# A graph network's tensor product laid out contiguously, with PSUM operands in the scoring and placing stages

## The chip, the cores and the metric

One core of a Trainium2 chip runs the whole kernel. The metric is the device time of one execution in microseconds (us). The kernel before takes 12370.3 us, the median of three runs (12365.73 to 12378.43).

The engines are named as in the profile: PE (TensorE, with its weight loads as PEld), DVE (VectorE), ACT (ScalarE), POOL (GpSimd) and SP (SyncE). POOL issues the indirect DMAs; SP and ACT issue the plain ones.

## The reference, cut to what matters

Four graph layers work on 12500 nodes with 32 features and on 200000 edges sorted by `dst`. Before each layer `h = relu(layernorm(x))`, and the layer's result is added to `x`.

```
# layer 0: scores of edges, two heads of 32
en, ev = (h @ W2s + b2s)[src], (h @ W2d + b2d)[dst]
e      = sum(leaky_relu(en + ev, 0.2) * attn, -1)
alpha  = softmax of e over the edges of one dst
msg    = softmax(en * r_feat * alpha, -1)
x     += (h + sum over heads(segment_sum(msg, dst))) @ W1 + b1
# layer 1
x     += segment_sum(h[src], dst)
# layer 2: weights of a tensor product per edge, MUL = 8
tpw = silu(silu(radial @ W1 + b1) @ W2 + b2) @ W3 + b3      # 4 blocks of 8 x 8: W00, W110, W01, W10
m0  = a * (einsum('eu,euw->ew', hs*sh0, W00) + einsum('eui,ei,euw->ew', hv, sh1, W110)/sqrt(3))
m1  = a * (einsum('eu,ei,euw->ewi', hs, sh1, W01) + einsum('eui,euw->ewi', hv*sh0, W10))
x  += self terms + segment_sum([m0, m1], dst) / 4
# layer 3: attention with four heads over the edges of one src
```

Layer 3 sums over `src`, so the kernel also puts the edges in the order of `src`.

## The kernel before, in words

The 200000 edges are padded to 128 x 1568: partition p holds 1568 edges that follow each other. An edge stage goes through them in 98 chunks of 16 columns (CH = 16), two chunks k = 0, 1 to a turn of the loop, each with its own buffers. A stage is a block of five programs, one per engine, which wait for each other by semaphores that count chunks. The order of the work is written out by hand in each `body`. Stages don't overlap. Each gather or scatter of one column is one indirect DMA on POOL's queue, 16 for a chunk and 1568 for a stage.

**Scoring stage (lines 809 to 1000).** POOL gathers rows of `tab_s0` (L864) into `en`; SP stores them (L850); ACT loads them back (`bring`, L876) with the rows of `dst`, which are written once per node (L645) and spread over the edges of the node by a running scan (`Spread`, L623 to 677). DVE first counts `dst` with one-hot comparisons against a row of iotas (`count_dst`, `hot`, L938 and L940), which PE adds up; from that come the positions that L645 needs (`starts`). POOL gathers 12 turns before it waits for them. Then DVE's loop (L981) makes, for each chunk, the one-hot rows of `src`, the scan (L675), the add (L988), the leaky ReLU (L989), the product with `attn` (L990) and the sum (L991). POOL's loop waits for the loaded indices and for SP's store two chunks before, not for DVE.

**Placing stage (L1003 to L1273).** DVE multiplies `en` by `r` (L1233), weights it (L1239), takes a softmax per head (maximum L1244, subtraction L1248, ACT's exponential, sum L1199, product L1203), adds the heads into `fresh` (L1207) and scans (L603). In the same loop PE ranks the edges by `src` from one-hot rows (`hot`, L1191 and L1193), DVE picks the ranks (L1217), and POOL scatters the edge's ends to their place (L1060). DVE's `send` waits until the scatters of two chunks before have landed, as it writes their buffers; POOL waits for `posed` (L1227).

**Sum stage (L1333 to L1440).** POOL gathers `tab_h` rows (L1314), ACT turns them into `fresh`, which is in PSUM here, and DVE scans. The weights of layer 2 are prepared beside it.

**Tensor-product stage (L1449 to L1696).** The same L1314 gathers `tab_h` rows; PE makes the 256 weights of each edge in four quarters of a chunk (L1526 and L1527, double buffered in `tp_ps`); DVE multiplies them in PSUM by the edge's vectors (`prod_a` L1661, `prod_b` L1664) and reduces (`res_a` L1647, `res_b` L1649). `prod_b` is laid out so that its reduction reads with a step of 8 elements. `prepare` and `dot` make the vectors `zv` (L1621), `zz` (L1623, L1631) and `hv1` (L1624); ACT widens `zv` (L1578) and copies `hs` (L1574). The messages are added in turned order into `fresh` in SBUF (L1688, L1692) and scanned (L603) a chunk later. POOL waits for `prepared` and `widened` of two chunks before.

**Attention stage (L1850 to L1963).** POOL gathers `tab_h3` rows (L1876); the message `fresh`, and with it one input of the long scan, is in PSUM.

Of the kernel before, what the change touches and what calls it, by code (L numbers as in the profile page):

```python
# [113 lines left out]
def known_ge(t, n):  # L114

    return isinstance(t, int) and t >= n
# [15 lines left out]
def build(nc, A, out):  # L132
    top = ExitStack()
    with top:
# [115 lines left out]
        class EdgeMasks:  # L250
# [11 lines left out]
            def scratch(self, st, ends=None):  # L262
# [12 lines left out]
                self.rows = ps(st, "rows", [128, 2, 512])  # L275
# [346 lines left out]
        class Spread:  # L622
# [4 lines left out]
            def __init__(self, st, width, table, masks):  # L627
                self.masks = masks
                self.width, self.whole, self.table = width, table, edge_rows(table[0:EDGES, :])
                self.raw = [sb(st, f"raw{k}", [EP, CH, width]) for k in range(2)]  # L630
                self.fresh = [sb(st, f"sfresh{k}", [EP, width, CH + 1]) for k in range(2)]
                self.keep = [sb(st, f"skeep{k}", [EP, width, CH + 1]) for k in range(2)]
                self.run = [sb(st, f"srun{k}", [EP, width, CH + 1]) for k in range(2)]
# [18 lines left out]
            def start(self):  # L652

                for k in range(2):
                    last = nc.vector.memset(self.keep[k][:, :, 0], 0.0)
                return [last, nc.vector.tensor_copy(self.run[1][:, :, CH], self.init[:, :])]
# [5 lines left out]
            def lay(self, act, t, k, i):  # L662
# [4 lines left out]
                K.wait(act, "act", self.raw_in[k], i * 16 + 16)  # L667
                nc.scalar.copy(self.fresh[k][:, :, 1:CH + 1], self.raw[k][:, :, :].rearrange("p c f -> p f c")).then_inc(self.laid, 1)  # L668

            def scan(self, dve, c, t, k):  # L670

                c.step(nc.vector.tensor_copy(self.fresh[k][:, :, 0], self.run[1 - k][:, :, CH]))
# [4 lines left out]
                K.wait(dve, "dve", self.spread, t + 1)  # L677

# [130 lines left out]
        with ExitStack() as st:  # L809
# [7 lines left out]
            zw = sb(st, "zw", [EP, CH, 64])  # L817
# [6 lines left out]
            cnt_ps = [ps(st, f"cnt_ps{k}", [NP, NB]) for k in range(2)]  # L824
            tot_ps = ps(st, "tot_ps", [NP, NB])
            pre_ps = ps(st, "pre_ps", [NP, NB])
            ev = Spread(st, 64, ev_rows, by_dst)
            by_dst.scratch(st, dst_ends)
# [5 lines left out]
            cleared, scored, hots, counted, copied, summed, starts, chain_v, loaded = (  # L834
                K.sem(n) for n in ("cleared", "scored", "hots", "counted", "copied", "summed", "starts", "chain_v", "loaded"))
# [37 lines left out]
            def _(act):  # L873
# [32 lines left out]
            def _(pe):  # L906
                by_dst.turn(pe)
                for q in range(2):
                    nc.tensor.matmul(cnt_ps[q][:, :], zbias[:, :], zbias[:, 0:NB], start=True, stop=False)
# [1108 lines left out]
```

## Time and profile before

| What | Value |
|---|---|
| Median of three runs | 12370.3 us |
| Profiled execution | 12366.65 us, its span 12364.9 us |
| POOL busy | 9229.0 us, 75% of the span |
| DVE busy | 6714.3 us, 54% |
| PE, PEld, ACT busy | 3621.8, 2317.2, 3298.7 us |
| L1314 indirect DMAs, two stages | 3136, 3142.1 us, mean 1002 ns |
| L864 indirect DMAs, scoring | 1568, 2088.0 us, mean 1332 ns |
| L1060 indirect DMAs, placing | 1568, 1933.5 us, mean 1233 ns |
| L1876 indirect DMAs, attention | 1568, 1481.3 us, mean 945 ns |

Times of rows are from one profiled execution. A POOL row of an indirect DMA is the time in which POOL works on the instruction; 0.30 us lie between two of them. DVE rows that follow each other overlap by about 0.1 us, so the busy time of a stretch is less than the sum of its rows.

### The profile page before, as it was taken

What the parts mean: (1) busy time and instruction counts of PE and PEld (TensorE: products, weight loads), DVE (VectorE), ACT (ScalarE), POOL (GpSimd) and SP (SyncE); (2) the same over time, 40 slices, a digit from 0 to 9 for tenths busy, and PEclk for the clock granted to TensorE, in tenths of its full rate; (3) what the DMA queues carried; (4) which work ended last, traced back from release to release, by engine and by line L of the source; (5) the groups of instructions that cost most, each with busy time, mean ns of one, the idle gap of its engine ahead of it and who ended that gap; (6) DMA issues with size and microseconds to landing.
All of it is one profiled execution on the core that took longest, in us unless ns stands there. A gap on an engine that the chain in (4) does not pass through costs nothing. (4 is left out here: it accounts for less than half of the span.)

```text
span 12364.9 us, 102503 instructions
## 1 busy us (share of the span) xinstructions
PE 3621.8 (29%) x22342; PEld 2317.2 (19%) x22342; DVE 6714.3 (54%) x9984; ACT 3298.7 (27%) x4609; POOL 9229.0 (75%) x8449
## 2 busy tenths in 40 slices
PE   3201000004555555510000000778887710000002
PEld 2200000003555545510000000233333210000001
DVE  8628754547666666630000001999999914444443
ACT  0002111113444444411111110333333303343332
POOL 5878877774777777767777776777777667777775
PEclk6555555556777777755555555888888755555555
DMA  6123322221111111111111111111111112222222
GB/s 231 41 61 112 96 82 88 83 85 52 52 56 52 54 53 52 56 22 27 26 26 27 26 26 33 27 27 27 27 27 27 25 14 71 71 71 74 71 71 60
DMA packets 596616, 683.05 MB, mean 55 GB/s; under 512 B 341381, under 2 KB 437478, under 8 KB 583766
## 3 DMA queue, kind: packets, MB, share of 16 engines
q0 software_dynamic: 270016, 149.13, 7.8%
q10 hardware_dynamic: 116464, 346.86, 7.6%
q1 hardware_dynamic: 210086, 186.52, 5.0%
q8 instruction: 16, 0.26, 0.0%
q14 instruction: 34, 0.28, 0.0%
HBM read 371.16 MB, written 310.60 MB: 55 GB/s over the span
## 5 line engine op out<-in xcount | busy, mean ns | idle before, releaser
L1314 POOL DMA_INDIRECT hs<-tab_h,idx x3136 | 3142.1, 1002 | 1047.1 <-issue 987.1
L864 POOL DMA_INDIRECT en<-tab_s,idx x1568 | 2088.0, 1332 | 582.8 <-issue 489.3
L1060 POOL DMA_INDIRECT by_src<-ends,pos_i x1568 | 1933.5, 1233 | 630.1 <-issue 495.1
L1876 POOL DMA_INDIRECT hs<-tab_h,idx x1568 | 1481.3, 945 | 511.8 <-issue 511.8
L1526 PE MATMUL tp_ps<-w_pair,x 128*128 128x512 f32 x1568 | 1010.3, 731 | 273.2 <-DVE prod_b L1664 272.9
L592 DVE COPY fresh<-run 128x32 f32<-128x32 f32 (+1 forms) x392 | 109.9, 280 | 1783.2 <-ACT fresh L1401 1768.4
L916 PE MATMUL cnt_ps<-hot_hi,hot_lo 128*128 128x98 bf16 x3136 | 287.3, 281 | 2409.2 <-DVE hot_hi L940 2409.2
L603 DVE TENSOR_TENSOR_SCAN run<-keep,fresh 128x544 f32<-128x544 f32 (+1 forms) x392 | 851.7, 2173 | 89.2 <-DVE fresh L592 58.3
L614 ACT COPY rows<-run 128x512 f32<-128x512 f32 (+1 forms) x392 | 706.9, 1803 | 516.0 <-DVE run L603 516.0
L916 PEld LDWEIGHTS cnt_ps<-hot_hi,hot_lo 128*128 128x128 bf16 x3136 | 250.6, 140 | 2445.9 <-issue 2059.1
L666 ACT COPY skeep<-cont_dst 128x1024 f32 (+1 forms) x98 | 102.4, 1045 | 2147.7 <-issue 2113.8
L1082 PE MATMUL rank_ps<-place_sb,hot_t 128*128 128x98 f32 x3136 | 661.6, 323 | 9.7 <-DVE picked L1217 9.4
L675 DVE TENSOR_TENSOR_SCAN srun<-skeep,sfresh 128x1088 f32<-128x1088 f32 (+1 forms) x196 | 268.3, 1369 | 685.1 <-ACT sfresh L668 653.2
L1757 PE MATMUL turn<-ident,both 128*33 128x128 f32 x8 | 1.9, 418 | 2155.4 <-DVEq L1787 2155.4
L1649 DVE TENSOR_REDUCE res_b<-prod_b 128x96 f32<-128x768 f32 x392 | 600.1, 1531 | 0.0
L529 PE MATMUL turn<-ident,tails 128*32 128x128 f32 x3 | 1.2, 394 | 2042.1 <-DMA tails<-sums 2042.1
L1082 PEld LDWEIGHTS rank_ps<-place_sb,hot_t 128*128 128x128 f32 x3136 | 542.3, 217 | 12.9 <-DVE picked L1217 6.6
L1137 ACT COPY hot_tb<-turn_ps 128x512 bf16<-128x512 bf16 x392 | 232.6, 593 | 1162.9 <-PE turn_ps L1072 1081.0
L1401 ACT COPY fresh<-hs 128x512 f32<-128x512 f32 x98 | 99.7, 1017 | 1409.5 <-DMA hs<-tab_h,idx 1409.5
L1941 DVE COPY score<-most 128x4 f32<-128x4 f32 x98 | 20.0, 204 | 838.7 <-DMA hs<-tab_h,idx 838.7
L1072 PE MATMUL turn_ps<-identb,hot_lo 128*128 128x128 bf16 x1568 | 174.4, 243 | 1016.7 <-DVE hot_hi L1193 1016.7
L1757 PEld LDWEIGHTS turn<-ident,both 128*33 128x33 f32 x8 | 1.2, 169 | 2155.7 <-DVEq L1787 2155.5
(327 smaller groups left out, 12998.4 us busy)
## 6 DMA issues: line engine op xcount, KB each, us to landing
sums<-rows ACTq DMA_DIRECT2D x98, 1088.0 KB
sums<-rows ACTq DMA_DIRECT2D x294, 256.0 KB
hs<-tab_h,idx POOLq DMA_INDIRECT x4704, 2.4
ev_rows<-zeros ACTq DMA_DIRECT2D x16, 3136.0 KB, 9.9
en_rows<-en SPq DMA_DIRECT2D x98, 512.0 KB
en_back<-en_rows ACTq DMA_DIRECT2D x98, 512.0 KB, 3.8
raw<-ev_rows ACTq DMA_DIRECT2D x98, 512.0 KB
en<-en_rows SPq DMA_DIRECT2D x98, 512.0 KB
```

Source lines behind the costliest of these rows:

```text
L603: nc.vector.tensor_tensor_scan(flat(self.run[k]), flat(self.keep[k]), flat(self.fresh[k]), 0.0, ALU.mult, ALU.add).then_inc(self.scanned, 1)
L614: nc.scalar.copy(self.rows[k][:, :, 0:self.width], self.run[k][:, :, 1:CH + 1].rearrange("p f c -> p c f")).then_inc(self.copied, 1)
L675: nc.vector.tensor_tensor_scan(flat(self.run[k]), flat(self.keep[k]), flat(self.fresh[k]), 0.0, ALU.mult, ALU.add).then_inc(self.spread, 1)
L864: pool.indirect_dma_start(en[k][:, g, :], None, tab_s0, bass.IndirectOffsetOnAxis(ap=idx[k][:, g:g + 1], axis=0)).then_inc(gathered[k], 16)
L916: last = nc.tensor.matmul(cnt_ps[q][:, :], hot_lo[k][:, g, :], hot_hi[k][:, g, :], start=False, stop=False)
L1060: pool.indirect_dma_start(by_src, bass.IndirectOffsetOnAxis(ap=pos_i[k][:, g:g + 1], axis=0), ends[k][:, g, :], None).then_inc(sent[k], 16)
L1082: nc.tensor.matmul(o, hot_t[q][:, b, :], place_sb[q][:, :], start=True, stop=False)
L1137: nc.scalar.copy(hot_tb[q][:, :, :], turn_ps[q % 2][:, :, 0:EP])
L1314: pool.indirect_dma_start(rows[k][:, g, :], None, tab_h, bass.IndirectOffsetOnAxis(ap=idx[k][:, g:g + 1], axis=0)).then_inc(gathered[k], 16)
L1526: nc.tensor.matmul(o, x2[k][:, a, b * EP:(b + 1) * EP], w3[:, :, :].rearrange("p o n -> p (o n)"), start=True, stop=False)
L1649: c.link(nc.vector.tensor_reduce(res_b[:, four, :, :].rearrange("p c i w -> p (c i) w"), prod_b[q % 2][:, :, :, :, :].rearrange("p c i u w ...
L1876: pool.indirect_dma_start(rows[k][:, g, :], None, tab_h3, bass.IndirectOffsetOnAxis(ap=idx[k][:, g, 1:2], axis=0)).then_inc(gathered[k], 16)
```

## The change

Three things are changed together.

*Scoring stage.* `zw` moves to PSUM. The row of iotas is copied to a PSUM tile once, as f32, and the comparisons read it there. `Spread` gets a form with one PSUM tile that is `fresh` and `run` at once for both chunks: the scan writes over its input, `free` carries the last column to the first, and ACT lays the next chunk only after that (`freed`). The leaky ReLU is split: ACT multiplies `zw` by 0.2 into `fifth` (`added`, `tilted`), and DVE takes the maximum. The comparisons of a chunk move behind the add. To have the banks, the counts share one bank, as do `tot_ps` and `pre_ps`, and the edge masks use `zw`'s.

*Placing stage.* A PSUM tile of one bank holds the iotas, `z_top`, `z_div` and a copy of the chunk's weights. `turn_ps` has one buffer instead of two. The heads are added by a reduction over the head instead of an addition.

*Tensor-product stage.* The weights `w3` and `b3` are turned once, so that an edge's 256 weights come as [w][block][u]. Both products and all reductions then read and write contiguously: `prod_a` is [w][24], `prod_b` is [w][i][u] and is made from `zv` without the widened copy. `res_a` is split into a reduction that writes m0 directly and one for `res_p`. The message is added in plain order into `msg`, and ACT turns it into `fresh` (`lay`). `prepare` moves to the end of a chunk, and PE's order of transposition, hidden layers and products changes.

```diff
@@ class Spread
+                if psum:
+                    held = ps(st, "sheld", [EP, -(-width * (CH + 1) // 512) * 512])
+                    whole = held[:, 0:width * (CH + 1)].rearrange("p (f c) -> p f c", c=CH + 1)
+                    self.fresh = self.run = [whole, whole]
+                    self.freed = K.sem("spread_freed")
...
+                if self.psum:
+                    K.wait(act, "act", self.freed, t + 1)
                 nc.scalar.copy(self.fresh[k][:, :, 1:CH + 1], self.raw[k][:, :, :].rearrange("p c f -> p f c")).then_inc(self.laid, 1)
...
+            def free(self, dve):
+                nc.vector.tensor_copy(self.fresh[0][:, :, 0], self.run[0][:, :, CH]).then_inc(self.freed, 1)
@@ scoring: ACT, then DVE
+                        K.wait(act, "act", added, t + 1)
+                        nc.scalar.mul(fifth[:, :, :], zw[:, :, :], 0.2).then_inc(tilted, 1)
                         if not known_ge(t, 2 * PAIRS - 1):
                             ev.lay(act, t + 1, 1 - k, i + k)
...
-                    nc.vector.tensor_tensor(hot_lo[k][:, :, :], iota_row[0:EP, :].unsqueeze(1).to_broadcast([EP, CH, 128]),
+                    nc.vector.tensor_tensor(hot_lo[k][:, :, :], iota_ps[:, 0:128].unsqueeze(1).to_broadcast([EP, CH, 128]),
...
-                        hot(lo_s, hi_s, t, k)
                         ev.scan(dve, c, t, k)
                         K.wait(dve, "dve", back_in[k], i * 16 + 16)
                         c.step(nc.vector.tensor_tensor(zw[:, :, :], en_back[k][:, :, :], ev.rows(k), ALU.add))
-                        c.step(nc.vector.scalar_tensor_tensor(zw[:, :, :], zw[:, :, :], 0.2, zw[:, :, :], ALU.mult, ALU.max))
+                        dve.sem_inc(added, 1)
+                        ev.free(dve)
+                        hot(lo_s, hi_s, t, k)
+                        K.wait(dve, "dve", tilted, t + 1)
+                        c.step(nc.vector.tensor_tensor(zw[:, :, :], zw[:, :, :], fifth[:, :, :], ALU.max))
@@ placing
+            small_ps = ps(st, "small_ps", [EP, 512])
+            per_edge = lambda at: small_ps[:, at:at + CH * HEADS0].rearrange("p (c h) -> p c h", h=HEADS0)
+            iota_ps, z_top, z_div, weight = small_ps[:, 0:128], per_edge(128), per_edge(160), per_edge(192)
...
-                    K.wait(pe, "pe", turned_sb, n - 1)
+                    K.wait(pe, "pe", turned_sb, n)
...
-                    c.link(nc.vector.tensor_tensor(S.message(k), z[k][:, :, 0:FEAT].rearrange("p c f -> p f c"),
-                                                   z[k][:, :, FEAT:2 * FEAT].rearrange("p c f -> p f c"), ALU.add))
+                    c.link(nc.vector.tensor_reduce(S.message(k), z[k][:, :, :].rearrange("p c (h f) -> p f c h", h=HEADS0), AX.X, ALU.add))
@@ tensor product: ACT
+                def lay(t, k):
+                    K.wait(act, "act", messaged, t + 1)
+                    K.wait(act, "act", S.scanned, t - 1)
+                    nc.scalar.copy(S.message(k), msg[k][:, :, :].rearrange("p c f -> p f c")).then_inc(laid, 1)
@@ tensor product: DVE
+                            a, b = prod_a[q % 2], prod_b[q % 2]
+                            c.link(nc.vector.tensor_reduce(msg[k][:, four, 0:MUL], a[:, :, :, 0:2 * MUL], AX.X, ALU.add))
+                            c.link(nc.vector.tensor_reduce(res_p[:, four, :], a[:, :, :, 2 * MUL:3 * MUL], AX.X, ALU.add))
+                            return c.mark(nc.vector.tensor_reduce(res_q[:, four, :].rearrange("p c n -> p (c n)"),
+                                                                  b[:, :, :, :].rearrange("p n i u -> p (n i) u"), AX.X, ALU.add))
...
+                        nc.vector.tensor_tensor(msg[k][:, :, MUL:FEAT], cross[:, :, :, :].rearrange("p c w i -> p c (w i)"),
+                                                res_q[:, :, :], ALU.add).then_inc(messaged, 1)
+                        if more:
+                            prepare(c, t + 1, 1 - k, i + k)
```

## Rows read from the trace of the kernel before

**Rows 1.** The page's first part: busy us, share of the span, instructions.
```profile
PE 3621.8 (29%) x22342; PEld 2317.2 (19%) x22342; DVE 6714.3 (54%) x9984; ACT 3298.7 (27%) x4609; POOL 9229.0 (75%) x8449
```

**Rows 2.** Stretches, POOL's gathers alone: length, busy; scoring twice, sum stage.
```profile
92.00:722.00 630.00, 508.77 (x384) 0.50 0.37 126
849.00:2800.00 1951.00, 1578.62 (x1184) 0.50 0.31 92
...
5534.00:7517.00 1983.00, 1482.83 (x1568) 0.50 0.13 27
```

**Rows 3.** Stretches, all engines: PE, PEld, DVE, ACT, POOL; counting, placing, tensor product.
```profile
112.00:495.00 383.00, 142.34 (x1555) 124.25 (x1556) 382.68 (x196) 0.00 (x0) 322.89 (x195) 0.50 0.44 159
2934.00:5363.00 2429.00, 1381.66 (x13928) 1237.09 (x13927) 1627.14 (x4562) 1168.06 (x2224) 1933.47 (x1568) 0.77 0.17 52
7687.00:9846.00 2159.00, 1737.72 (x4391) 673.93 (x4391) 2054.27 (x2416) 720.32 (x878) 1659.22 (x1568) 0.86 0.13 27
```

**Rows 4.** Timeline in scoring: start, duration, engine, line.
```profile
1602.83 2.29 DVE L938 TENSOR_TENSOR hot_lo<-iota_row,lo_s 128x2048 bf16<-128x2048 bf16 x1 [0.54 <-remote]
1603.31 2.63 POOL L864 DMA_INDIRECT en<-tab_s,idx  x1 [0.30 <-issue]
...
1625.27 0.94 POOL L864 DMA_INDIRECT en<-tab_s,idx  x1 [0.30 <-issue]
1625.43 1.23 DVE L990 TENSOR_TENSOR zw<-zw,attn 128x1024 f32<-128x1024 f32 x1
```

**Rows 5.** Timeline in the tensor-product stage; `fresh` in SBUF.
```profile
8601.17 1.28 DVE L603 TENSOR_TENSOR_SCAN run<-keep,fresh 128x544 f32<-128x544 f32 x1
8601.36 1.85 POOL L1314 DMA_INDIRECT hs<-tab_h,idx  x1 [0.30 <-issue]
```

**Rows 6.** Timeline in the attention stage; `fresh` in PSUM.
```profile
11016.98 4.83 DVE L603 TENSOR_TENSOR_SCAN run<-keep,fresh 128x2244 f32<-128x2244 f32 x1 [0.28 <-DVE fresh L592]
11017.72 0.94 POOL L1876 DMA_INDIRECT hs<-tab_h,idx  x1 [0.30 <-issue]
```

**Rows 7.** Timeline in the placing stage, POOL and DVE alone.
```profile
4023.12 1.29 DVE L603 TENSOR_TENSOR_SCAN run<-keep,fresh 128x544 f32<-128x544 f32 x1 [0.29 <-DVE fresh L1207]
4023.99 1.20 POOL L1060 DMA_INDIRECT by_src<-ends,pos_i  x1 [0.30 <-issue]
4025.24 1.22 DVE L1233 TENSOR_TENSOR z<-en,r 128x1024 f32<-128x1024 f32 x1 [0.82 <-remote]
4025.49 1.81 POOL L1060 DMA_INDIRECT by_src<-ends,pos_i  x1 [0.30 <-issue]
4027.61 0.97 POOL L1060 DMA_INDIRECT by_src<-ends,pos_i  x1 [0.30 <-issue]
```

**Rows 8.** Stretches, scoring's reduction L991 alone: length, busy, count of chunks.
```profile
850.00:1420.00 570.00, 50.07 (x41) 0.50 0.36 111
850.00:2820.00 1970.00, 119.68 (x98) 0.50 0.31 92
```

**Rows 9.** Instruction groups by line and shape: busy us, mean ns of one, idle before.
```profile
L1649 DVE TENSOR_REDUCE res_b<-prod_b 128x96 f32<-128x768 f32 x392 | 600.1, 1531 | 0.0
L1647 DVE TENSOR_REDUCE res_a<-prod_a 128x96 f32<-128x768 f32 x392 | 368.6, 940 | 0.0
L938 DVE TENSOR_TENSOR hot_lo<-iota_row,lo_s 128x2048 bf16<-128x2048 bf16 x98 | 224.6, 2292 | 65.3 <-remote 64.5 <-DVE zw L990 0.5
L668 ACT COPY sfresh<-raw 128x1024 f32<-128x1024 f32 x98 | 190.7, 1946 | 298.7 <-DMA raw<-ev_rows 298.7
L1692 DVE TENSOR_TENSOR fresh<-cross,res_b 128x384 f32<-128x384 f32 x98 | 107.2, 1094 | 0.0
L1207 DVE TENSOR_TENSOR fresh<-z 128x512 f32<-128x512 f32 x98 | 102.9, 1050 | 0.0
```

**Rows 10.** Waits of DVE in the placing stage: us in total, times, longest.
```profile
DVE ends L1223 <- DMA by_src<-ends,pos_i: 641.4, 95, 9.9
```

**Rows 11.** The page's DMA issues: KB each, median us from issue to landing.
```profile
en_back<-en_rows ACTq DMA_DIRECT2D x98, 512.0 KB, 3.8
```

More of the change, by code:

```diff
@@ L260, in __init__, with scratch @@
                 self.fwd_all = sb(top, "fwd_all_" + name, [128, EP])
-            def scratch(self, st, ends=None):
+            def scratch(self, st, ends=None, rows=None):
                 self.ends = ends
@@ L655, in start @@
                     last = nc.vector.memset(self.keep[k][:, :, 0], 0.0)
-                return [last, nc.vector.tensor_copy(self.run[1][:, :, CH], self.init[:, :])]
+                first = self.fresh[0][:, :, 0] if self.psum else self.run[1][:, :, CH]
+                return [last, nc.vector.tensor_copy(first, self.init[:, :])]
             def load(self, eng, t, k):
@@ L1024, in build @@
             place_ps = ps(st, "place_ps", [NP, NB])
-            turn_ps = [ps(st, f"turn_ps{k}", [NP, GR, 128], BF16) for k in range(2)]
+            turn_ps = ps(st, "turn_ps", [NP, GR, 128], BF16)
             own_ps = ps(st, "own_ps", [EP, GR, EP])
@@ L1324, in build @@
         w2 = sb(weights, "w2_pair", [128, 128])
-        w3 = sb(weights, "w3_pair", [128, 2, TPW])
+        w3 = sb(weights, "w3_pair", [128, 2, MUL, 4, MUL])
         b1 = sb(weights, "b1_pair", [128, 1])
@@ L1493, in body @@
                         K.wait(pool, "pool", prepared, t - 1)
-                        K.wait(pool, "pool", widened, t - 1)
+                        K.wait(pool, "pool", copied_hs, t - 1)
                         gather(pool, t, k, i)
@@ L1583, in _ @@
                 layer2(0, 0)
-                widen(0, 0, 0)
+                copy_hs(0, 0, 0)
+                S.mask(act, 0, 0)
                 def body(i):
@@ L1639, in body @@
                         c, last_c = chains[k], chains[1 - k]
-                        K.wait(dve, "dve", widened, t + 1)
+                        more = not known_ge(t, 2 * PAIRS - 1)
                         def total(q, done):
@@ L1668, in body @@
+                            nc.vector.tensor_tensor(
+                                prod_b[q % 2][:, :, :, :],
+                                wts[:, :, :, 3 * MUL:].rearrange("p c w u -> p (c w) u").unsqueeze(2).to_broadcast([EP, 4 * MUL, 3, MUL]),
+                                zv[k][:, four, :, :].rearrange("p c i u -> p c (i u)").unsqueeze(2).to_broadcast([EP, 4, MUL, 3 * MUL]),
+                                ALU.mult).then_inc(taken, 1)
                             if q == 1:
                                 last_c.restart()
-                            if q == 1 and not first_chunk(t):
-                                S.scan(dve, c, t - 1, 1 - k, carried=True, settle=False)
@@ L1684, in body @@
-                        crossed = c.mark(nc.vector.tensor_tensor(cross[:, :, :, :], sh1(t), res_a[:, :, :, 2].unsqueeze(3).to_broadcast([EP, CH, MUL, 3]), ALU.mult))
-                        msg = S.message(k)
+                                if not first_chunk(t):
+                                    K.wait(dve, "dve", laid, t)
+                                    S.scan(dve, c, t - 1, 1 - k, carried=True, settle=False)
+                            if q == 0:
+                                K.wait(dve, "dve", laid, t - 1)
+                            else:
+                                summed[q - 1] = total(q - 1, made[q - 1])
```

211 lines of the change are left out of this document (102 added, 109 removed).

## Prediction

> **What bounds the kernel now.** I read the page's first part, then a table of engine times for each stage, then the instruction groups of the POOL queue, then the timeline around the long members of those groups. POOL is busy 75% of the span, VectorE 54% [rows 1]. POOL's work is 98 chunks of 16 indirect DMAs in each of five stages: gathering for scoring (L864), scattering in the placing stage (L1060), gathers of the sum stage and of the tensor-product stage (both L1314), and of the attention stage (L1876). The 1568 gathers of the sum stage need 1983 us [rows 2], 1.26 us each and 20.2 us a chunk. They need 630 + 1951 = 2581 us in scoring [rows 2], 2429 us in placing and 2159 us in the tensor-product stage [rows 3]. So in three stages POOL is slower than its own clean pace, and nothing in its rows says that it waited: the rows are longer.
>
> The timeline shows why. A gather is 0.94 us. The one that starts at 1603.31, inside the VectorE comparison of 1602.83 to 1605.12, lasts 2.63 us and ends 0.82 us after it; the one at 1625.27, which has already begun when a product starts at 1625.43, lasts 0.94 us [rows 4]. The scan at 8601.17 stretches the gather at 8601.36 to 1.85 us [rows 5]. What these VectorE rows share is two inputs in SBUF. In the attention stage the scan of 4.83 us takes one input from PSUM, and a gather that starts inside it lasts 0.94 us [rows 6]. So a VectorE instruction with two SBUF inputs holds POOL at a point some 0.1 us into an indirect DMA until it ends; one with an input in PSUM does not.
>
> The excess is the difference of POOL's busy times over the same 1568 instructions: scoring 508.8 + 1578.6 - 1482.8 = 605 us [rows 2]; tensor product 1659.2 - 1482.8 = 176 us [rows 2, 3]; placing, whose unheld scatter is 0.97 us [rows 7], 1933.5 - 1568 x 0.969 = 414 us.
>
> **The change, part by part. Scoring.** The one-hot comparisons read the iota from PSUM, the scan works in place in one PSUM tile, the add reads its result there, and the leaky ReLU becomes an ACT product into SBUF and a maximum of that with PSUM. Every large VectorE instruction of the loops then has a PSUM input, in the first counting loop too. Of the 605 us I keep 5 us for the mask scans before the loops and take 600. POOL waits there for nothing of VectorE but `starts`. The counting loop costs 3.9 us a chunk (383 us for 98) [rows 3] and ends at 495; POOL reaches the placing of rows at 722 minus its excess of 508.8 - 384 x 0.945 = 146, about 580, so `starts` is still early. VectorE then begins scoring 146 us sooner, at about 704, and while it is behind it does 41 chunks in 570 us, 13.9 us each [rows 8]: 704 + 98 x 13.9 = 2066, before POOL's end at 2800 - 600 = 2200. POOL stays the bound up to 15.3 us a chunk. The added ACT product (1024 elements, at most the 1.95 us of the turned copy L668 [rows 9]) stands beside the comparisons, which are now issued behind the add: 4 us of them stand between the add and the maximum. Only in the last chunk are they exposed, since they used to run while its data was fetched: +4 us. Net -596.
>
> At one place a rule of the Trainium skill would speak against this. The all-bf16 comparison of 2048 elements takes 2292 ns, 1.12 ns an element [rows 9]; the f32 product of 1024 elements takes 1.22 us [rows 7], 1.19 ns an element, so the bf16 one has no faster mode now. VectorE: DVE Perf Modes, section "Why PSUM operands drop a tier", has it that an operand in PSUM takes the faster modes away from an instruction; by that rule the pair of comparisons would cost twice as much if it ran in such a mode now. By the row it doesn't, and the sum has 0 for it; the doubled pair is priced as a rival below.
>
> **Placing.** The comparisons, the weighting, the subtraction of the maximum and the division get a PSUM input, the head sum becomes a reduction with one input, and a small copy of the weights is added. Two holders are left: the product L1233 and the scan L603. In the timeline they cost 1.20 - 0.97 = 0.23 and 1.81 - 0.97 = 0.84 us [rows 7]. The 0.23 is luck of phase: other holders ran just in front. Against a stream with a point every 1.27 us, a lone holder of 1.29 us costs 0 to 1.29, 0.65 on average; one of 1.22 us that follows by 0.83 us then costs 0.8. I take 1.45 us a chunk, 142 us, between 50 (both fall well) and 210 (both fully). Saved: 414 - 142 = 272.
> VectorE must follow. It waits 641 us for landed scatters in this stage, 6.5 us a chunk [rows 10]; its loop is 2429 / 98 = 24.8, less 6.5, 18.3 us. The weights' copy adds 0.2. The head sum of 1024 strided elements replaces 1.05 us [rows 9]; strided reduction of 768 elements costs 1.53 us (L1649), contiguous 0.94 (L1647) [rows 9], so 1024 cost 1.2 to 2.1; I take 2.0. Loop: 19.5 us, against POOL's (2429 - 272) / 98 = 22.0. POOL keeps the bound by 2.5 us. The single turn_ps costs nothing: each transposition waits for ACT's copies of the group before, issued a group earlier.
>
> **Tensor product.** VectorE is busy 2054 / 98 = 21.0 us a chunk, in a stage whose chunk is 22.0 [rows 3]. The strided reduction goes from 1.53 to 0.94 us, four times: -2.4. Splitting the other into 512 and 256 elements adds four fixed parts of about 0.1: +0.4. The strided message add of 1.09 us [rows 9] becomes a contiguous one of about 0.55, and the add of a third as many elements beside it goes, by the same row some 0.36: -0.9. VectorE: 18.1. But POOL was nearly the bound already: 20.2 clean + 1.8 excess = 22.0. So VectorE's 3 us are worth only what they let POOL have. The scan (both inputs in SBUF, up to 1.29) stays; the long add is replaced by a short one; the products of `prepare` and the cross product stay. Per chunk: scan 0.65, the short ones 0.65, together 1.3 (0.4 to 2.2) against 1.8: -0.5 x 98 = -49. ACT loses the widened copy and gains the turned message copy; both lie beside. The stage's tail (last landing to last scan) is one VectorE chunk either way: -1. Extra weight turning in the sum stage is hidden by its gathers: 0. Net -50.
>
> **Sum**, on the profiled execution's 12366.65 (span 12364.9 and 1.75 around it): -596 - 272 - 50 = -918, 11449. The median before is 3.6 above that execution: 11452.
>
> **Rivals.**
> (a) Holders left over fall well: 50 us in placing (-92 more), 0.5 us a chunk in the tensor product (-78 more): 11282. For it: scan 0.23 [rows 7]. Against: the two are adjacent and cannot both be missed often. 0.10.
> (b) VectorE, or its chain with PE and ACT, becomes the bound: placing at 24 us a chunk (reduction dearer, turn_ps serialising) gives 98 x 2.0 = +196; tensor product gains nothing, +50: 11698. For it: margins of 2.5 us; PE is busy 1738 us of 2159 there [rows 3]. Against: waits of VectorE for PE are almost absent. 0.10.
> (c) The comparisons double (the page's rule above): counting ends at 878, `starts` holds POOL until 885 instead of 580, and scoring runs at 13.9 + 4.1 = 18.0: 885 + 124 (placing rows) + 98 x 18 = 2773 against a forecast of 2220: +553; placing at 23.6, +157: 12162. Against: rows 9. 0.03.
> (d) The change doesn't do what it says: a PSUM input doesn't release POOL for comparisons whose other input is broadcast from SBUF, or in-place writing holds it. Then only about 50 is gained, and 4 lost: 12324. Against: rows 6. 0.03.
> (e) Slower: scoring has one tile where there were two for input and two for result, so scan, add, freeing, ACT's product, ACT's copy and the fetch of the next chunk can become one serial ring, with ACT standing behind its own `bring`. Fully serial: VectorE 13.9 + three ACT instructions of at most 1.95 + fetch 3.8 [rows 11] + store, taken the same, 3.8 = 27.4 us a chunk: 704 + 98 x 27.4 = 3389, 569 after the 2820 of now [rows 8]; less 272 and 50: 12617. It makes the kernel slower from (2820 + 322 - 704) / 98 = 24.9 us a chunk. Against: the next chunk's copy needs only add and freeing, so ring and comparisons overlap. 0.03.
> (f) The forecast: 0.71, with 11370 to 11540 of its own.
>
> A measurement tells 0.2%, 25 us, from no change. Faster: (a), (b), (c), (d), (f), 0.96 after something for what I overlook; same 0.01; slower 0.03. The range reaches over most of (a)'s and part of (b)'s way: 11330 to 11600.
>
> **What would show it.** Right: L864 at 0.95 us in the mean, L1060 near 1.06, the tensor product's gathers near 1.03; no gather stretched by a row with a PSUM input; VectorE idle on gathered rows in the tensor product, 3 us a chunk; its wait for scatters in placing down from 641 to about 250 us. Wrong: POOL rows of 0.95 us with idle time on `posed`, `prepared` or `starts` between (b, c, e), comparisons of over 2.3 us (c), long gathers inside comparisons (d).

## The result, and the profile after

The kernel after takes 11331.1 us (median of four runs, 11329.1 to 11339.1) against 12374.3 for the kernel before on the same chip: the ratio is 0.916, with a 95% interval of 0.914 to 0.918. It saves 1043 us; the forecast was 918, and its own range 11370 to 11540 was missed by 39 us, the wide one (11330 to 11600) reached by 1 us.

The page's first part and its groups of POOL's indirect DMAs, after (lines have moved: L864 is L881, L1060 is L1086, L1314 is L1342):

```profile
PE 3517.1 (31%) x22342; PEld 2369.0 (21%) x22342; DVE 6460.4 (57%) x10384; ACT 3225.0 (28%) x4707; POOL 8175.6 (72%) x8449
...
L1342 POOL DMA_INDIRECT hs<-tab_h,idx x3136 | 3035.4, 968 | 1046.2 <-issue 997.0
L1086 POOL DMA_INDIRECT by_src<-ends,pos_i x1568 | 1587.1, 1012 | 654.6 <-issue 513.8
L881 POOL DMA_INDIRECT en<-tab_s,idx x1568 | 1486.5, 948 | 590.6 <-issue 492.3
```

POOL is busy 9229.0 - 8175.6 = 1053 us less [rows 1], and the kernel is 1043 us shorter, with as many instructions on POOL. Scoring's gathers fell from 1332 to 948 ns in the mean, the scatters from 1233 to 1012.

Stretches of after in the order of [rows 3], all engines: scoring, placing, tensor product. After the length come PE, PEld, DVE, ACT and POOL, then the granted clock of PE as a share of 2.4 GHz, the busy share of the DMA engines and GB/s.

```profile
90.00:2206.00 2116.00, 288.39 (x3124) 251.63 (x3125) 1507.49 (x1013) 366.08 (x290) 1582.38 (x1667) 0.50 0.40 124
2344.00:4448.00 2104.00, 1387.73 (x13931) 1241.20 (x13928) 1726.15 (x4658) 1169.81 (x2224) 1587.11 (x1568) 0.81 0.20 60
6772.00:8823.00 2051.00, 1635.60 (x4398) 726.24 (x4398) 1788.36 (x2715) 568.25 (x878) 1552.35 (x1568) 0.85 0.13 28
```

| Stage: first to last indirect DMA | before, us | after, us | saved | forecast |
|---|---|---|---|---|
| scoring | 2707.0 | 2114.9 | 592 | 600 |
| gap from there to placing | 134.8 | 138.6 | -4 | -4 |
| placing | 2428.9 | 2103.1 | 326 | 272 |
| tensor product | 2158.1 | 2050.1 | 108 | 49 |
| from there to the attention stage's first gather | 331.0 | 324.3 | 7 | 1 |

The sum and attention stages kept 1982 and 1993 us. These differences add up to 1029 us, and the spans of the two profiled executions, 12364.9 and 11337.4, differ by 1028. The medians differ by 1043, because the execution profiled before lies 8 us under its kernel's median and the one profiled after 8 us over it.

Timeline of after in scoring (start, duration, engine, line), the place that answers to [rows 4]:

```profile
1812.94 2.43 DVE L686 TENSOR_TENSOR_SCAN sheld<-skeep,sheld 128x1088 f32<-128x1088 f32 x1 [1.23 <-ACT sheld L678]
1813.66 0.94 POOL L881 DMA_INDIRECT en<-tab_s,idx  x1 [0.30 <-issue]
...
1817.14 2.29 DVE L958 TENSOR_TENSOR hot_lo<-iota_ps,lo_s 128x2048 bf16<-128x2048 f32 x1
1817.41 0.94 POOL L881 DMA_INDIRECT en<-tab_s,idx  x1 [0.30 <-issue]
1818.65 0.94 POOL L881 DMA_INDIRECT en<-tab_s,idx  x1 [0.30 <-issue]
```

The gather that starts inside the scan of 2.43 us and the two inside the comparison of 2.29 us last 0.94 us, where the comparison of before made one of 2.63.

Timeline of after in placing, POOL and DVE alone, an odd chunk (the second of a turn of the loop) and an even one (the first of a turn), for [rows 7]:

```profile
3304.94 1.29 DVE L603 TENSOR_TENSOR_SCAN run<-keep,fresh 128x544 f32<-128x544 f32 x1 [0.36 <-DVE fresh L1234]
3305.78 1.23 POOL L1086 DMA_INDIRECT by_src<-ends,pos_i  x1 [0.30 <-issue]
3306.68 1.22 DVE L1260 TENSOR_TENSOR z<-en,r 128x1024 f32<-128x1024 f32 x1
3307.32 1.42 POOL L1086 DMA_INDIRECT by_src<-ends,pos_i  x1 [0.30 <-issue]
...
3327.69 1.29 DVE L603 TENSOR_TENSOR_SCAN run<-keep,fresh 128x544 f32<-128x544 f32 x1 [0.29 <-DVE fresh L1234]
3328.14 1.62 POOL L1086 DMA_INDIRECT by_src<-ends,pos_i  x1 [0.30 <-issue]
3330.06 0.97 POOL L1086 DMA_INDIRECT by_src<-ends,pos_i  x1 [0.30 <-issue]
3330.07 1.25 DVE L1260 TENSOR_TENSOR z<-en,r 128x1024 f32<-128x1024 f32 x1
```

In the odd chunk z<-en,r starts 0.45 us after the scan's end and stretches a scatter by 0.45 us. In the even one it starts 1.09 us after the scan's end, 0.01 us behind a scatter, which stays at 0.97.

Timeline of after in the tensor product, for [rows 5]:

```profile
7615.58 1.28 DVE L603 TENSOR_TENSOR_SCAN run<-keep,fresh 128x544 f32<-128x544 f32 x1
7616.03 1.58 POOL L1342 DMA_INDIRECT hs<-tab_h,idx  x1 [0.30 <-issue]
```

Groups of after by line and shape (busy us, mean ns), for [rows 9]:

```profile
L1691 DVE TENSOR_REDUCE res_q<-prod_b 128x96 f32<-128x768 f32 x392 | 369.2, 942 | 0.0
L1689 DVE TENSOR_REDUCE msg<-prod_a 128x32 f32<-128x512 f32 x392 | 263.0, 671 | 0.0
L958 DVE TENSOR_TENSOR hot_lo<-iota_ps,lo_s 128x2048 bf16<-128x2048 f32 x98 | 224.1, 2287 | 0.0
L1234 DVE TENSOR_REDUCE fresh<-z 128x512 f32<-128x1024 f32 x98 | 190.0, 1939 | 0.0
L1690 DVE TENSOR_REDUCE res_p<-prod_a 128x32 f32<-128x256 f32 x392 | 159.9, 408 | 0.0
L1008 DVE TENSOR_TENSOR zw<-en_back,sheld 128x1024 f32<-128x1024 f32 x98 | 120.5, 1229 | 28.7 <-DVE sheld L686 28.7
L1727 DVE TENSOR_TENSOR msg<-cross,res_q 128x384 f32<-128x384 f32 x98 | 55.0, 561 | 0.0
```

Waits of DVE in after: us in total, times, longest. The first is of the placing stage, for [rows 10], the others of the tensor product:

```profile
DVE ends L1249 <- DMA by_src<-ends,pos_i: 215.4, 52, 7.5
...
DVE hv L1667 <- DMA hs<-tab_h,idx: 127.2, 78, 32.2
DVE prod_a L1704 <- PE tp_ps L1566: 88.4, 133, 1.1
```

### The profile page after: what moved, and what is told of

It is laid out like the page before. It is cut to its first block and busy times, and to the rows that moved or that the text cites. A ratio compares the mean times of both kernels' runs of the same rounds, so it can differ in the third digit from the quotient of the medians.

```text
span 11337.4 us, 103348 instructions
## 1 busy us (share of the span) xinstructions
PE 3517.1 (31%) x22342; PEld 2369.0 (21%) x22342; DVE 6460.4 (57%) x10384; ACT 3225.0 (28%) x4707; POOL 8175.6 (72%) x8449
## 5 line engine op out<-in xcount | busy, mean ns | idle before, releaser
L1342 POOL DMA_INDIRECT hs<-tab_h,idx x3136 | 3035.4, 968 | 1046.2 <-issue 997.0
L1086 POOL DMA_INDIRECT by_src<-ends,pos_i x1568 | 1587.1, 1012 | 654.6 <-issue 513.8
L881 POOL DMA_INDIRECT en<-tab_s,idx x1568 | 1486.5, 948 | 590.6 <-issue 492.3
L1913 POOL DMA_INDIRECT hs<-tab_h,idx x1568 | 1481.4, 945 | 511.7 <-issue 511.7
L1565 PE MATMUL tp_ps<-w_pair,x 128*128 128x512 f32 x1568 | 905.4, 661 | 6.5 <-DVE prod_b L1707 6.5
L1549 PE MATMUL hid_ps<-radial_t,w_pairs 128*128 128x128 f32 x1568 | 357.4, 420 | 413.5 <-ACT radial_t L1597 413.5
L1704 DVE TENSOR_TENSOR prod_a<-tp_ps,zz 128x768 f32<-128x768 f32 x392 | 374.3, 955 | 136.6 <-PE tp_ps L1566 90.1
L1549 PEld LDWEIGHTS hid_ps<-radial_t,w_pairs 128*128 128x128 f32 x1568 | 333.0, 323 | 439.9 <-issue 421.3
```

The source lines that it names most:

```text
L881: pool.indirect_dma_start(en[k][:, g, :], None, tab_s0, bass.IndirectOffsetOnAxis(ap=idx[k][:, g:g + 1], axis=0)).then_inc(gathered[k], 16)
L1086: pool.indirect_dma_start(by_src, bass.IndirectOffsetOnAxis(ap=pos_i[k][:, g:g + 1], axis=0), ends[k][:, g, :], None).then_inc(sent[k], 16)
L1342: pool.indirect_dma_start(rows[k][:, g, :], None, tab_h, bass.IndirectOffsetOnAxis(ap=idx[k][:, g:g + 1], axis=0)).then_inc(gathered[k], 16)
L1549: last = nc.tensor.matmul(hid_ps[:, a, b * EP:(b + 1) * EP], w1[:, a * 4 + b, :], radial_t[:, :], start=True, stop=True)
L1565: nc.tensor.matmul(o, x2[k][:, a, b * EP:(b + 1) * EP], w3_cols, start=True, stop=False)
L1704: made[q] = c.mark(nc.vector.tensor_tensor(prod_a[q % 2][:, :, :, :], wts[:, :, :, 0:3 * MUL], zz[k][:, four, :, :].rearrange("p c n u -> ...
```

## The experiments

In all of them the "hold" of a VectorE line is worked out from the trace: for each indirect DMA what it lasts above 0.944 us (gather) or 0.969 us (scatter), put down to the large VectorE instruction that ended about 0.8 us before it. In the table of the parts a saving is the difference to the kernel before in the same session; elsewhere medians of different sessions are compared. The kernel before had medians of 12371.3 to 12378.5 us in the five sessions, so such a difference is uncertain by some 7 us. Line numbers are each kernel's own. Where the text speaks of an odd or an even chunk, the first chunk of a stage is even.

**The three parts, each alone** on the kernel before. Their edits are the parts of the diff: scoring with counting; placing; tensor product.

> The kernel before with the scoring part alone. Holding theory (a VectorE row with two SBUF inputs holds POOL's indirect DMA, and only POOL's time counts): the whole 600 us of excess go, +4 us behind the last gather: 12374 - 590 = 11784 (+-15), placing and tensor product to the microsecond as before. Rival (the gain is shorter VectorE work: the add fell from 1.97 to 1.23 us, the scan's copies moved): VectorE's loop was not what the stage waited for, so the rival has to expect well under 100 us: 12270 or more.

> The kernel before with the placing part alone. Holding theory: what the trace of the changed kernel shows for this stage comes alone as well, 2429 to 2103 us: 12374 - 326 = 12048 (+-15). Rival (the three parts help each other, for example by the memory traffic they leave): clearly less than 326.

> The kernel before with the tensor-product part alone. Holding theory: gathers of the stage 2158 to 2050 us and 7 us at its end: 12374 - 115 = 12259 (+-15). If the three parts are independent, the three savings of these runs add up to the 1043 of the whole within 20 us.

| Part alone | median, us | ratio, 95% | saved | its stage's length, us |
|---|---|---|---|---|
| scoring | 11783.1 | 0.952 (0.951 to 0.954) | 594 | 2114.2 |
| placing | 12101.5 | 0.978 (0.976 to 0.980) | 276 | 2157.3 |
| tensor product | 12258.9 | 0.990 (0.989 to 0.992) | 118 | 2048.2 |

Scoring and tensor product save alone what they save together. Placing doesn't: it misses its expectation by 53 us, its stage is 54 us longer alone, and the three savings make 988 us, 55 short of 1043 where 20 were allowed. In the holds one line differs: z<-en,r has 67.5 us over 93 chunks alone and 23.3 over 50 in the kernel after; the scan has 45 us in both. Timeline of placing alone, an even chunk:

```profile
3896.85 1.29 DVE L603 TENSOR_TENSOR_SCAN run<-keep,fresh 128x544 f32<-128x544 f32 x1 [0.29 <-DVE fresh L1210]
3897.79 1.14 POOL L1062 DMA_INDIRECT by_src<-ends,pos_i  x1 [0.30 <-issue]
3899.19 1.21 DVE L1236 TENSOR_TENSOR z<-en,r 128x1024 f32<-128x1024 f32 x1
3899.23 2.02 POOL L1062 DMA_INDIRECT by_src<-ends,pos_i  x1 [0.30 <-issue]
```

Here z<-en,r starts 1.05 us after the scan's end (1.04 in nearly all even chunks), 0.04 us ahead of the scatter, and holds it 1.05 us. In the kernel after the same instruction comes 0.05 us later, behind the scatter's start. In both kernels the copy of the weights starts 0.94 us after the scan's end; z<-en,r follows it after 0.10 us alone and after 0.15 us in the kernel after. An experiment on that stands below.

**Iota back in SBUF.** The kernel after, with one operand of scoring's four comparisons read from SBUF again:

```diff
-nc.vector.tensor_tensor(hot_lo[k][:, :, :], iota_ps[:, 0:128]...
+nc.vector.tensor_tensor(hot_lo[k][:, :, :], iota_row[0:EP, :]...
-nc.vector.tensor_tensor(hot_hi[k][:, :, :], iota_ps[:, 0:NB]...
+nc.vector.tensor_tensor(hot_hi[k][:, :, :], iota_row[0:EP, 0:NB]...
```

> The changed kernel, but scoring's comparisons read the iotas from SBUF (bf16) as before; nothing else differs, and the comparisons take the same 2.28 and 1.78 us either way. Holding theory: POOL is held again, in the counting loop and in the scoring loop: a lone holder of 2.29 us costs 1.67, the one behind it some 0.5, in 196 chunks 350 to 425 us: 11331 + 390 = 11720, gathers of scoring back to a mean near 1190 ns. Rival (length or order of VectorE's work made the gain): no change, 11331.

Measured: 11657.3 us, ratio 0.942 (0.940 to 0.943), 326 us more than after, which is 24 less than the least that was expected. Scoring's gathers are 1804.1 us busy instead of 1486.5, the stage 2428.5 us long. Timeline:

```profile
1616.97 2.35 DVE L958 TENSOR_TENSOR hot_lo<-iota_row,lo_s 128x2048 bf16<-128x2048 bf16 x1
1618.25 1.89 POOL L881 DMA_INDIRECT en<-tab_s,idx  x1 [0.30 <-issue]
1619.24 1.78 DVE L960 TENSOR_TENSOR hot_hi<-iota_row,hi_s 128x1568 bf16<-128x1568 bf16 x1
1620.44 1.40 POOL L881 DMA_INDIRECT en<-tab_s,idx  x1 [0.30 <-issue]
```

The comparisons last as long as with PSUM (2305 against 2287 ns in the mean), VectorE does the same work, and 317 us of hold are back on them alone. The edit also turns the operand from f32 back to bf16, but the type doesn't decide: z<-en,r, all f32 and in SBUF, holds scatters, and scoring's add with the same type and one operand in PSUM (L1008) holds none of the gathers that start inside it. So it is the place of the operand that stretches the gathers.

**A later scan in placing.** The kernel after, with a reduction that nobody needs ahead of the stage's scan, in three sizes:

```diff
+c.link(nc.vector.tensor_reduce(idle_out[:, :], idle_in[:, 0:288], AX.X, ALU.add))   # 576, 864
 S.scan(dve, c, t, k, carried=True)
```

> The changed kernel with one more VectorE reduction (288 elements of SBUF, one input, about 0.35 us in the chain) before the scan of the placing stage. VectorE has 2.2 us a chunk to spare there. Locked theory (VectorE starts each chunk at the landing of a scatter, so its holders fall at a fixed place of POOL's rhythm of 1.27 us): the scan's hold, 0.46 us a chunk on average now, moves with the delay, up by about 0.35 or over the edge to near 0: stage 2103 + 34 or - 45, so the total moves by 20 to 50 us either way. Random theory (holders fall anywhere): 0, within 15 us: 11331.

> As the run with 288 elements, with 576: about 0.65 us later. Locked theory: another point on a sawtooth with period 1.27 us and height 1.29 us a chunk (126 us over the stage), different from the neighbours by 20 us or more. Random theory: 11331 within 15.

> As before, with 864 elements: about 0.95 us later. Locked theory: a third point of the sawtooth; over the four delays 0, 0.35, 0.65 and 0.95 the stage spreads by 50 to 120 us. Random theory: 11331 within 15. If VectorE became the bound instead, the total would rise with each step by 0.3 us x 98 = 30 us and POOL would show idle time on posed.

| Elements (mean ns) | median, us | stage, us | hold of scan | hold of z<-en,r |
|---|---|---|---|---|
| none | 11331.1 | 2103.1 | 44.8 | 23.3 |
| 288 (439) | 11328.6 (11321.5 to 11330.7) | 2105.9 | 62.2 | 24.9 |
| 576 (738) | 11316.7 (11307.2 to 11324.6) | 2092.4 | 46.8 | 20.0 |
| 864 (1039) | 11293.0 (11289.4 to 11300.3) | 2066.2 | 21.4 | 24.1 |

With VectorE busy 102 us more, the kernel is 38 us shorter. If the scan started anywhere against the scatters, its hold would be about the same in all four kernels; it is 45, 62, 47 and 21 us, so it depends on the delay. The locked theory missed as well: the first step moved the total by 3 us instead of 20 or more, and the stage spreads by 40 us (2105.9 to 2066.2), not 50 to 120. Nor is the scan at a fixed place. In the kernel before it held 0.23 and 0.31 us in turns; in the kernel after the hold lies anywhere between 0 and 1.03 us from chunk to chunk. VectorE waits for landed scatters in every second chunk, which couples it to POOL, but how the places of the scan come about isn't worked out.

The hold isn't the whole gain either. Of the 37 us that the last stage is shorter, POOL's rows gave 23. The other 14 are POOL's idle time at the start of a chunk: beyond the 0.30 us between two scatters it waits 13 times, once every 112 scatters, 38 us in all in the kernel after and 24 here. What makes these waits come every 112 scatters, no run shows.

**More work in the tensor product.** The kernel after, with 2304 elements reduced for nobody behind the last reduction of each chunk:

```diff
 summed[3] = total(3, made[3])
+c.link(nc.vector.tensor_reduce(idle_out[:, :], idle_in[:, :], AX.X, ALU.add))
```

> The changed kernel with one more VectorE reduction (2304 elements of SBUF, one input, about 2.4 us) in every chunk of the tensor product, which gives back most of the 2.9 us by which the contiguous layout shortened VectorE's chunk. Holding theory (POOL bounds the stage; only the holders' time counts): the stage stays at 2050 us but for the phase, +-40: 11331 (11290 to 11375). Rival (the shorter VectorE work made the gain of this stage): +2.4 x 98 = 235 us less what was idle, so the 115 us come back: 11440 or more.

Measured: 11450.4 us, ratio 0.925 (0.923 to 0.926), 119 more than after: the rival's figure. Stretch of its tensor-product stage (all engines), its group of the filler, and POOL's waits there:

```profile
6774.00:8924.00 2150.00, 1624.44 (x4355) 724.38 (x4356) 1991.18 (x2787) 559.90 (x872) 1569.21 (x1568) 0.85 0.11 27
...
L1725 DVE TENSOR_REDUCE idle_out<-idle_in 128x1 f32<-128x2304 f32 x96 | 244.3, 2544 | 0.0
...
POOL hs L1342 <- DVE zz L1675: 59.1, 25, 2.4
```

POOL's own time rose by 17 us only; it now waits for `prepared`, 59 us by name, and its idle time beyond 0.30 us a gather rose by 83. VectorE waits for gathered rows only once, at the stage's start (29.3 us), where it had waited 78 times. So VectorE's chain sets the pace, at 2149.5 / 98 = 21.9 us a chunk. The filler takes 2.4 us of it (2.54 less the overlap of 0.1), so without the filler the chain needs about 19.5, against POOL's 20.9: an estimated margin of 1.4 us. For this stage the theory that only the holders' time counts is refuted: VectorE's chain is close enough behind that a longer one takes the gain away.

**z<-en,r moved behind the scatter.** Placing alone, with one reduction of 64 elements ahead of z<-en,r in the even chunks:

```diff
+if k == 0:
+    c.link(nc.vector.tensor_reduce(idle_out[:, :], idle_in[:, 0:64], AX.X, ALU.add))
 nc.vector.tensor_tensor(z[k][:, :, :], en[k][:, :, :], r[k][:, :, :], ALU.mult)...
```

> The kernel before with the placing stage's change alone (12101.5 us), and one reduction of 64 elements (some 0.1 us) between the copy of the weights and z<-en,r, in every second chunk. With that stage alone z<-en,r starts 1.04 us after the scan's end in every second chunk, 0.04 us before the next scatter, and holds it 1.05 us; in the kernel after it starts 1.09 us after the scan's end, 0.01 us behind the scatter, and holds nothing. Theory: that is the whole difference of about 50 us between this stage alone and in the three together, so 0.1 us more work on VectorE makes the kernel faster by 46 times 1.05 us: 12055 us (12035 to 12070). Rival: the difference is another one (the stage's start, the tables' rows), and the filler is hidden or costs its own time: 12101 to 12110 us.

Measured: 12058.6 us (12041.7 to 12066.4), ratio 0.974 (0.973 to 0.976): 43 us less than placing alone. Timeline, an even chunk:

```profile
3931.38 1.29 DVE L603 TENSOR_TENSOR_SCAN run<-keep,fresh 128x544 f32<-128x544 f32 x1 [0.28 <-DVE fresh L1213]
3931.67 1.78 POOL L1064 DMA_INDIRECT by_src<-ends,pos_i  x1 [0.30 <-issue]
3933.71 0.21 DVE L1240 TENSOR_REDUCE idle_out<-idle_in 128x1 f32<-128x64 f32 x1
3933.76 0.97 POOL L1064 DMA_INDIRECT by_src<-ends,pos_i  x1 [0.30 <-issue]
3933.84 1.22 DVE L1241 TENSOR_TENSOR z<-en,r 128x1024 f32<-128x1024 f32 x1
```

z<-en,r now starts 1.17 us after the scan's end and is behind the scatter. The stage is 2106.9 us long, within 4 us of the one in the kernel after, and z<-en,r's hold is 22.6 us. An instruction of 0.13 us of added time, 49 times, took 43 us off, inside the theory's range. In the profiled executions the stage is 50 us shorter, and z<-en,r's hold is 45 of them. So this one place explains most of the 55 us by which the parts don't add up.

**z<-en,r later in odd chunks too.** The kernel after, with the four selections issued first where k is 1:

```diff
+if k == 1:
+    pick(t * GROUPS - 1, 1 - k, GROUPS - 1)
 K.wait(dve, "dve", rows_in[k], i * 32 + 32)
...
 if not first_chunk(t):
-    pick(t * GROUPS - 1, 1 - k, GROUPS - 1)
+    if k == 0:
+        pick(t * GROUPS - 1, 1 - k, GROUPS - 1)
```

> The kernel after, with the four selections of the chunk before issued ahead of z<-en,r in every odd chunk of the placing stage. There z<-en,r starts 0.45 us after the scan's end, 0.63 us before the next scatter, and holds it 0.46 us, 47 times. Theory: four selections (0.17 us apart) move it some 0.7 us later, to 1.15 us after the scan's end, behind the scatter's start at 1.08 us, where it holds nobody: 11331 less 22 us is 11309 us (11300 to 11322). Rival: later work in the chunk moves as well and is met elsewhere, or z falls 0.05 us short and holds a whole 1.05 us: 11331 to 11360 us.

Measured: 11334.5 us, ratio 0.916 (0.915 to 0.917), which is the kernel after's and inside the rival's range. POOL in the placing stage, in the kernel after and here:

```profile
2344.00:4448.00 2104.00, 1587.11 (x1568) 0.81 0.20 60
...
2346.00:4429.00 2083.00, 1582.47 (x1568) 0.81 0.20 61
```

z<-en,r starts 1.36 us after the scan's end in odd chunks, and its hold there falls from 21 to 5 us. But the scan's hold rises from 45 to 50 and that of z<-en,r in even chunks from 2 to 8, so POOL's rows are only 5 us shorter. The profiled stage, 2081.5 us, is 22 us shorter because POOL's waits at the start of a chunk fell by 17, which the theory didn't have. That execution (11322.0) was the fastest of five; the other four took 11332 to 11336. The edit moved one holder as planned, the others took the hold over, and a gain in time is not shown.

**The tensor product's scan with a PSUM input.** The kernel after, with 30 of the 32 channels of `fresh` in the one bank that is free there, and the scan in two:

```diff
+head = ps(st, "fresh_head", [EP, split, CH + 1])      # split = 30
+self.parts = [[(0, split, head), (split, width, self.fresh[k])] for k in range(2)]
...
-nc.vector.tensor_tensor_scan(flat(self.run[k]), flat(self.keep[k]), flat(self.fresh[k]), 0.0,
+for a, b, part in self.parts[k] if self.split else [(0, self.width, self.fresh[k])]:
+    nc.vector.tensor_tensor_scan(flat(self.run[k][:, a:b]), flat(self.keep[k][:, a:b]), flat(part), 0.0,
```

The carry and ACT's message copy are in two likewise, and ACT waits for the scan of one chunk before instead of two.

> The kernel after, with the segment scan of the tensor product reading its message from PSUM: 510 of its 544 elements from one PSUM bank, the last 34 (two of 32 channels) in a second short scan from SBUF. In the trace of after this scan still holds the gathers for 52.8 us over 96 chunks (1.28 us each time it runs). Theory: with a PSUM operand it holds nobody, the short scan next to nothing, and the stage falls from 2050 to about 2000 us: 11281 us (11265 to 11305). Rival: VectorE already sets the stage's pace nearly as much as the gathers do (19.6 us a chunk by the filler's experiment, two instructions more here), and less than 25 us is gained: 11306 us or more. That the gather's time lies elsewhere: 11331 us.

Measured: 11300.6 us (11288.6 to 11306.8), ratio 0.913 (0.912 to 0.915): 31 us less than after. The profiled stage is 2004.6 us, 45.5 less. Its two scans, the stretch of the stage for POOL, and the row that holds a gather now:

```profile
L612 DVE TENSOR_TENSOR_SCAN run<-keep,fresh_head 128x510 f32<-128x510 f32 x96 | 115.8, 1207 | 0.0
L612 DVE TENSOR_TENSOR_SCAN run<-keep,fresh 128x34 f32<-128x34 f32 x96 | 19.6, 204 | 0.0
...
6771.00:8777.00 2006.00, 1505.17 (x1568) 0.83 0.15 29
...
7611.42 0.67 DVE L1679 TENSOR_TENSOR zv<-hs,sh 128x384 f32<-128x384 f32 x1
7611.57 1.32 POOL L1351 DMA_INDIRECT hs<-tab_h,idx  x1 [0.30 <-issue]
```

The scan's 52.8 us of hold are gone. zv<-hs,sh, which held next to nothing in after, now holds 19.1 us, and cross, hv and msg hold 7 instead of 19: 47 us less in all, as POOL's busy time says (1552.35 to 1505.17). The stage's 45.5 us are near the theory's 50. The medians differ by only 31, which is still inside the theory's range (11265 to 11305), near its upper end. Of the difference 6 us went in the attention stage of the profiled execution (1999.0 against 1992.8), and the profiled execution of the kernel after lies 8 us over its own median. VectorE waits 40 us for gathered rows here, 32 of them at the stage's start, where it was 127: little is left in this stage before VectorE is the bound.

**Both.** The kernel after with the split scan and the filler of 864 elements.

> The two edits that gained, on the kernel after: the reduction of 864 elements ahead of the placing stage's scan (11293.0 us alone, 38 us less) and the tensor product's scan with its message in PSUM (11300.6 us alone, 31 us less). They lie in different stages, so if each stage's pace is its own, the gains add: 11262 us (11245 to 11280). Rival: the placing stage's gain hangs on how the chunks happen to fall against the scatters and not on the edit, and comes out otherwise in another build: 11285 to 11325 us.

Measured: 11259.9 us (11257.3 to 11264.3), ratio 0.910 (0.909 to 0.911), the fastest of all: 71 us less than after, where 38 and 31 had been gained singly, and 2 us from the expectation. Its placing stage has 2065.5 us and its tensor product 2005.6, what each had alone.

## Why the prediction was right, and where its sizes were off

**What bounds it: right.** POOL's rows were long because VectorE instructions with two SBUF inputs held them. The experiment with the iota shows it by one operand's place. The sum was 125 us short: 54 of them lie in placing and 65 in the tensor product, 8 go the other way in scoring, and the rest is the distance of the profiled executions from the medians.

One detail of the mechanism was wrong. The prediction had the hold "at a point some 0.1 us into an indirect DMA". In the placing stage of the kernel after, z<-en,r starts some 0.01 us behind a scatter's start 42 times, and none of these scatters is stretched. With placing alone it starts some 0.04 us ahead 42 times, and each time the scatter is held. So the start of the DMA decides; what is left of the DMA after the holder's end is 0.75 to 0.84 us instead of the whole 0.94 or 0.97.

**Scoring, -596: measured -588** (592 for the stage, 4 back in the gap). Every gather of the scoring loop takes 0.94 to 0.96 us. The exposed tail of 4 us came as worked out: in the last chunk the comparisons stand between the add and the maximum. VectorE kept up: it waits 239.9 us in all for ACT's product (the group of L1013 names ACT fifth L917), at no cost, as POOL waits for none of this.

**The doubling (rival c): refuted.** With an f32 operand in PSUM the comparison takes 2287 ns where it took 2292 [rows 9]. The rule of the Trainium skill on operands in PSUM (VectorE: DVE Perf Modes, "Why PSUM operands drop a tier") took nothing away here: there was no faster mode to lose.

**Placing, -272: measured -326.** The mechanism held, the term of the two holders was mis-sized: 1.45 us a chunk, 142 us, became 68 (scan 44.8 and z<-en,r 23.3; 414 - 68 = 346, the fall of POOL's busy time), while POOL's waits beyond the 0.30 us between two scatters rose from 18 to 38 us. The scan's 0.65 a chunk came out as 0.46; the 0.23 that was called luck of phase had stood in every second chunk of before, with 0.31 in the others. The larger miss is z<-en,r, 0.8 taken and 0.24 found. "One of 1.22 us that follows by 0.83 us then costs 0.8" was the even chunk of before [rows 7]; it was carried over to all chunks and to a kernel in which the added copy of the weights stands between the two. In the trace of before z<-en,r starts 0.82 us after the scan in even chunks (held 0.84, 45 times) and 0.26 after it in odd ones (0.28, 47 times), some 52 us in all. In after, with the copy in front of it, these are 1.09 and 0.45. The next scatter after a scan that held one starts 1.08 us after the scan's end (0.78 to finish, 0.30 between), so one is missed by 0.01 us and the other costs 0.45. The copy was priced at 0.2 us of VectorE time; what counts is that z<-en,r now starts behind a scatter's start, which spares some 45 times a full hold. With the same code alone it fell 0.05 us short, and the stage saved 272 us, the forecast's number by accident. What makes that 0.05 us, between the starts of the copy and of z<-en,r, isn't settled.

VectorE's side was right: it waits 215 us for landed scatters (forecast 250), its loop is (2103 - 215) / 98 = 19.3 us (forecast 19.5), the strided head sum 1939 ns (2.0).

**Tensor product, -50: measured -115** (108, and 7 in the tail, where the last chunk's chain ends 24.0 us after the last gather instead of 30.9), the other mis-sized term. The holders left were put at 1.3 us a chunk; they hold 0.73 (72 us: scan 52.8, cross 9.5, hv 4.9, msg 4.6), and before they held 179. The scan was put at 0.65 and is 0.54; "the short ones 0.65" are 0.2. An instruction of 0.56 to 0.67 us can fall between two points 1.25 us apart and in most chunks does. The terms of the work were right: the contiguous reduction 942 ns, the message add 561, the split reduction 671 + 408, which is 0.14 us more than one where 0.1 was taken. VectorE is busy 1788 / 98 = 18.2 us a chunk (forecast 18.1). But its wait for gathered rows is 127 us, 32 of them at the stage's start, so 1.0 us a chunk and not 3: the chain has waits that busy time doesn't show (88 us for PE among them, 0.8 before), and the filler puts the chain at about 19.5 us. "VectorE's 3 us are worth only what they let POOL have" stands, with an addition: with VectorE's chain at 21.9 us the stage can't run at 20.9, so the contiguous layout was needed for the holds' saving to arrive. How much of the 115 us each of the two gives on its own was not separated.

**Rivals.** (a), holders falling well, was put at 11282 with a chance of 0.10; the measured time lies between it and the forecast, nearer to (a): 68 us left in placing (it had 50) and 0.73 us a chunk in the tensor product (0.5). Its ground against, "the two are adjacent and cannot both be missed often", was wrong: the distance between the two is fixed, and in even chunks it lets the second fall behind a scatter's start. (b) is refuted for the kernel as it is, by margins of POOL over VectorE of 2.2 us (21.5 - 19.3) in placing and 1.4 in the tensor product. (d) is refuted by the scoring rows, in-place writing among them, (e) by POOL's rows of 0.95 us, between which it waits for no VectorE work but `starts`.

**What would show it.** Of the signs named, L881 at 0.948 us came as said; L1086 at 1.012 (named 1.06) and the tensor product's gathers at 1552.35 / 1568 = 0.990 (named 1.03) were already the two misses.

## What to carry to other kernels

Where one engine's rows grow longer without a wait, group them by length and look what ran on the others at their start; here one operand moved to PSUM was worth 326 us with no instruction less. What a remaining holder costs isn't a mean over random positions. Where it follows another holder at a fixed distance, its cost is read from the distances between starts, for each buffer of the loop apart, and a cheap instruction between the two can be worth more than its own time, either way. Where it has no fixed place, like the scan here, the cost changed with every kernel (21 to 62 us) and was only measured. A holder moved out of the way is worth its hold only if the others stay where they are. Before a stall of the bounding engine is counted as gained, the next engine's whole chain is to be measured, for example by a filler of known length, since its busy time leaves out its waits.

## What the runs showed of the hardware

- A VectorE instruction with two inputs, one of them in PSUM, let the indirect DMAs through: comparisons, products, maxima and scans, in place in PSUM too (2.43 us scan, gather 0.94 us). In the scoring stage of the kernel after 630 gathers start inside a comparison and 192 inside a scan, and the longest of them takes 0.96 us. So did reductions with their one input in SBUF (the filler of 2.54 us held none of the 143 gathers that started inside it).
- What starts first decides: z<-en,r 0.04 us ahead of a scatter cost 1.05 us, 0.01 us behind it nothing.
- A longer VectorE program made the kernel faster twice: 102 us of filler gave 38 us, 49 reductions of 64 elements gave 43 us.
- The add of scoring went from 1970 to 1229 ns when its turned operand (step of 17 elements) and its result moved from SBUF to PSUM. A turned reading from SBUF remains in the head sum, 1939 ns for 1024 elements, against 942 ns for 768 contiguous ones.
